# A two-part graph network on one core: transposed one-hots kept in DRAM, gathers and sums interleaved by tile, address registers loaded a group ahead

## The reference

```python
for _ in range(3):                                    # message layers, l = 0, 1, 2
    msg = silu([h[src], h[dst], edge_attr] @ W1e + b1e) @ W2e + b2e
    agg = segment_sum(msg, dst) / deg
    h = h + silu([h, agg] @ W1n + b1n) @ W2n + b2n
x = layernorm(x + h)
for W, root, b in three_relational_layers:            # l = 3, 4, 5
    seg = edge_type * n_nodes + dst
    agg = segment_sum(x[src], seg) / max(cnt, 1)
    x = x @ root + b + einsum('rni,rio->no', agg, W)  # relu after the first two
out = layernorm(x_before + x)
```

## Time and profile before

| | |
|---|---|
| median of three runs | 6398.9 us (6395.67 to 6404.14) |
| the profiled execution | 6410.94 us |
| its span in the profile | 6409.2 us |
| TensorE, VectorE busy | 5167.9 us (81%), 4519.1 us (71%) |
| ScalarE, GpSimd busy | 2721.7 us (42%), 3388.0 us (53%) |
| message layers, first gather to last sum | 765.2, 775.7 and 780.9 us |
| relational layers, likewise | 745.0, 744.5 us and a third like them |

### The profile page before, as it was taken

The page is one execution under the profiler, slowest core; times in us unless marked ns, Lnnn a source line. Parts: engine busy times, 40 slices in busy tenths (PEclk is TensorE's granted clock), DMA queues, the critical chain, the costliest instruction groups (busy, mean ns, idle before and its releaser), DMA issues.

```text
span 6409.2 us, 169000 instructions
## 1 busy us (share of the span) xinstructions
PE 5167.9 (81%) x47647; PEld 4403.8 (69%) x47651; DVE 4519.1 (71%) x10320; ACT 2721.7 (42%) x4966; POOL 3388.0 (53%) x4176
## 2 busy tenths in 40 slices
PE   3666666614888888888898888999889989899898
PEld 2444444414777767777677776888878888788887
DVE  6444444413777767767667776999969999699996
ACT  1111111124666655555555554444434444344443
POOL 1777777722555535555355553555535555355552
PEclk9999997557999999999999999999989999899997
DMA  8111111167655546555455552112211112111120
GB/s 301 29 29 29 29 29 29 29 185 208 170 168 169 170 120 169 164 165 169 121 156 168 167 168 80 57 56 57 56 34 56 57 56 57 33 57 56 56 57 26
DMA packets 376130, 639.85 MB, mean 100 GB/s; under 512 B 68352, under 2 KB 80980, under 8 KB 376075
## 3 DMA queue, kind: packets, MB, share of 16 engines
q1 hardware_dynamic: 335016, 610.44, 31.6%
q0 software_dynamic: 38400, 28.13, 2.5%
q10 hardware_dynamic: 2658, 0.51, 0.0%
HBM read 564.82 MB, written 73.22 MB: 100 GB/s over the span
## 4 chain that ended last, share of the span: by engine, by line
PE 62%; POOL 17%; issue 10%; DMA 4%; ACT 3%; another core or an unknown queue 2%; DVE 2%; POOLq 0%; SPq 0%; ACTq 0%; DVEq 0%
PE sums L870 18%; PE sums L884 15%; POOL recs L489 13%; PE gat L845 11%; PE gat L847 10%; PE gat L850 4%; POOL arena L502 3%; ACT arena L641 3%; DMA arena<-recs 2%; DMA recs<-arena 1%; PE gat L950 1%; PE gat L948 1%; PE sums L961 0%; DVE arena L1103 0%
## 5 line engine op out<-in xcount | busy, mean ns | idle before, releaser
L845 PE MATMUL gat<-table,arena 128*128 x7680 | 1918.5, 250 | 277.9 <-ACT arena L641 164.2
L502 POOL TENSOR_SCALAR arena<-iota_f,arena 128x128 f32<-128x128 f32 x1920 | 1268.5, 676 | 1315.0 <-PE sums L884 1129.1
L847 PE MATMUL gat<-table,arena 128*128 x7680 | 1924.2, 251 | 0.0
L870 PE MATMUL sums<-arena 128*128 128x192 bf16 x15360 | 1887.7, 246 | 2.0 <-DVE arena L1245 2.0
L1245 DVE TENSOR_SCALAR arena<-iota_s,meta_t 128x512 bf16<-128x512 int16 x3840 | 1531.9, 471 | 111.8 <-PE sums L870 111.8
L870 PEld LDWEIGHTS sums<-arena 128*128 128x128 bf16 x15360 | 1325.9, 98 | 2.6 <-DVE arena L1245 2.6
L641 ACT CAST arena<-gat 128x768 bf16<-128x768 f32 x960 | 767.2, 799 | 1128.1 <-PE gat L847 1128.1
L1209 DVE TENSOR_SCALAR arena<-arena,lane 128x1024 bf16<-128x1024 bf16 x1920 | 1058.1, 592 | 192.3 <-DMA arena<-rows_d 191.4
L489 POOL DMA_INDIRECT recs<-arena x800 | 950.4, 1188 | 381.0 <-issue 378.6
L884 PE MATMUL sums<-arena 128*128 128x64 f32 (+1 forms) x7680 | 959.6, 278 | 207.5 <-issue 142.2
L884 PEld LDWEIGHTS sums<-arena 128*128 128x128 f32 x7680 | 898.6, 192 | 309.7 <-issue 309.5
(11 more groups left out here) (181 smaller groups left out, 4799.9 us busy)
## 6 DMA issues: line engine op xcount, KB each, us to landing
arena<-rows_d SPq DMA_DIRECT2D x480, 512.0 KB, 4.5
arena<-recs SPq DMA_DIRECT2D x640, 272.0 KB, 2.8
arena<-rows_d SPq DMA_DIRECT2D x480, 256.0 KB, 3.3
recs<-arena SPq DMA_DIRECT2D x1, 43520.0 KB, 122.6
recs<-arena POOLq DMA_INDIRECT x800, 2.9
arena<-in_edge_attr_dram SPq DMA_DIRECT2D x100, 62.5 KB
xn<-in_x_dram SPq DMA_DIRECT2D x1, 768.0 KB
out_dram<-nodes SPq DMA_DIRECT2D x1, 768.0 KB
```

Of the source, the lines that this page charges most:

```text
L502: ins = pool.tensor_scalar(oh[u % 2][:, j, :], iota_f[:], rec_in[u][:, j, PLACE:PLACE + 1], None, ALU.is_equal)
L845: pe.matmul(at, ohT[s][:, 0, j * P:(j + 1) * P], table_flat[:, bass.ds(off[j], K3)], start=True, stop=False)
L847: ins = pe.matmul(at, ohT[s][:, 1, j * P:(j + 1) * P], table_next[:, bass.ds(off[j], K3)], start=False, stop=l >= LAYERS)
L870: ins = pe.matmul(accp[s][:, 256 * r:256 * r + K3], oh4[s][:, t, r * P:(r + 1) * P], gb[u % 4][:, t, :], start=t == 0, stop=t == GT - 1)
```

## The change

Transposed one-hots are made in layer 0 only. There SyncE stores each group's three (768 KB) to a new DRAM tensor `hots_d`, and in layers 1 to 5 it loads them instead of the rows: 768 KB per group in layers 1 and 2, 512 KB in layers 3 to 5. `ohT` has four buffers, `row_in` two. The one-hots by type and destination, `oh4`, have four buffers as well, so that `type_hots(g)` waits for the sums of `g - 4`.

TensorE runs the same `stage` in all layers: after the gathers of tile j of group g come the sums of tile j of group `g - 2`. The registers of group `g + 1` are loaded after tile 3 of group g (`load_gather`, `load_sums`), into two fixed sets. In message layers VectorE adds all three parts half by half, and the next gather waits for each half (`gat_read`) instead of for `z_ready`.

```diff
+            def store_hots(k, u):
+                sp.wait_ge(ohT_made, done(k))
+                sp.dma_start(hots_by_group[:, bass.ds(k, 1), :].rearrange("p a w -> p (a w)"),
+                             ohT[u].rearrange("p m e -> p (m e)")).then_inc(hots_stored[u], 16)
+            def load_hots(l, k, u):
+                m = 3 if l < LAYERS else 2
+                sp.wait_ge(gathered, done(2 * (l * NG + k - 4) + 1))
+                sp.dma_start(ohT[u][:, 0:m, :].rearrange("p m e -> p (m e)"),
+                             hots_by_group[:, bass.ds(k, 1), 0:m * GT * P].rearrange("p a w -> p (a w)")
+                             ).then_inc(hots_loaded[u], 16)
...
+                def load_gather(g, u, l=l):
+                    pe.load(tile_regs[u % 2], offsets[0:1, bass.ds(GT * g, GT)])
+                    if l < LAYERS:
+                        pe.load([dst_reg[u % 2]], goff[0:1, bass.ds(3 * g, 1)])
+                def load_sums(g, u, l=l):
+                    if l < LAYERS:
+                        pe.load([sum_reg[u % 2]], goff[0:1, bass.ds(3 * g + 1, 1)])
...
-                    pe.wait_ge(ohT_made, done(n))
-                    if l < LAYERS:
-                        pe.wait_ge(z_ready, done(n - 1))
...
+                    for j in range(GT):
+                        if gathers:
+                            gather_tile(g, u, j, off, dst_off)
+                        if adds:
+                            if j == 0:
+                                sums_ready(g - 2, (u + 2) % 4)
+                            sums_tile(g - 2, (u + 2) % 4, j, to)
+                        if j == 3:
+                            if gathers:
+                                load_gather(g + 1, u + 1)
+                            if not known or 1 <= g <= NG:
+                                load_sums(g - 1, u + 1)
...
-                    for k in range(1, 3):
-                        dve.wait_ge(z_step, 3 * n + 1 + k)
-                        ins = dve.tensor_tensor(z[s], z[s], parts[:, :, k * HID:(k + 1) * HID], ALU.add)
...
+                        dve.tensor_tensor(z[s][:, tiles, :], z[s][:, tiles, :], parts[:, tiles, HID:2 * HID], ALU.add
+                                          ).then_inc(z_step, 1)
+                        dve.wait_ge(z_step, 4 * n + 2 * h + 2)
+                        ins = dve.tensor_tensor(z[s][:, tiles, :], z[s][:, tiles, :], parts[:, tiles, 2 * HID:K3],
+                                                ALU.add)
+                        ins.then_inc(gat_read, 1)
...
-                    dve.wait_ge(summed, done(n - 2))
+                    dve.wait_ge(summed, done(n - 4))
```

329 lines of the change are left out of this document (172 added, 157 removed).

## The result

The changed kernel takes 6291.12 us (median of four runs, 6284.04 to 6295.09) against 6397.28 us before: a ratio of 0.9832, interval 0.9815 to 0.9849. It is faster, as forecast, but by 1.7% (106 us) and not by 314 us. The predicted time was 6085 us, and 6291 lies above the range of 5790 to 6195.

A forecast was written before the change was run, and what follows sets the result against it. VectorE was taken to bound relational layers and TensorE's sequencer, at or near its limit, message layers. Terms -306 - 32 + 18 + 6 = -314 us, from 6410.9 less 12 to the median, gave 6085 us; range 5790 to 6195.

The forecast's parts named there:

- Relational layers (-306: Layers 3 to 5: without transposed one-hots on VectorE, TensorE bounds at 4.01 us per group; -306 us over three layers.
- Layers 1 and 2 (-32: Message layers 1 and 2: sequencer still bounds, 4.65 us per group against 4.75; -16 us per layer, -32 us.
- A: The forecast: message layers unchanged or nearly so, relational layers bound by matmuls; 6085 us, 56%.
- B: Rival, message layers: register loads don't hold the sequencer, so 3.9 us per group; 5845 us, 26%.
- its sum closed on 4.67: Message group before: address instructions and register loads, with 0.82 us for the load of eight, add up to 4.67 us.
- Rival E: All layers: a register load costs by the register, eight taking 2.0 us; about 6830 us, slower, 3%.
- The prediction's sum by the 200 ns: Register loads at 200 ns per register: eight would take 1.6 us, kernel an estimated 6490 us; weighed and rejected.
- Layer 0 (+18: Layer 0: storing one-hots makes transfers the bound, 4.9 us per group; 783 us against 765, +18 us.
- part 3 of the change: Layer 0 still makes the one-hots and also stores them, 786,432 bytes per group; costed at +18 us.
- Loads of the one-hots in layers 1 and 2: Layers 1 and 2: DMA of 3.2 to 3.8 us within 4.65 per group, hidden by four buffers; cost 0.
- Rival D: Transfers bound the message layers: at 210 GB/s layer 0 +430 us, layers 1 and 2 +140; about 6640 us, 4%.
- Ends: +6: Message layers' ends: sums lag two groups, so each layer ends with one more sum alone, 2 us; +6 us in all.

## Why the prediction was right and where it was wrong

**Relational layers (-306, measured -323): right.** TensorE became the bound: busy 636.55 of 637.13 us, 3.98 us per group for 4.01, VectorE at 80%. Keeping VectorE busy brought 84 of the 108 us back; the rest of the gain is that it waits less. The load of eight was hidden at tile 3, as costed.

**Layers 1 and 2 (-32, measured -17): right on what a load does, and lucky in the sum.** That a load holds the sequencer was the open question between A and B; the records show it, and without the loads the layer takes 3.69 us per group, so it is A. But the saving was to be 0.1 us in each steady group, from 4.75 to 4.65. A steady group went from 4.74 to 4.78 us: the forecast counted the jump inside the 4.65, and with it the group is slower than before. What the layers gained lies elsewhere. Worked out from the starts of the gathers, the groups beside the regular ones cost about 10 and 14 us more in layers 1 and 2 before, where the granted clock dipped (0.98 and 0.97 of the whole window), and nothing after, at 1.00. The prediction named those dips, and did not count on their going.

The prices of the loads can be read from the records. In ns, where no stores run: 305 for one register, 546 for two, 597 for eight, 1082 for ten; and with the first word off a multiple of 16 bytes 1946 for eight and 2402 for ten. Around each load stand 0.12 us of set-up and 0.06 us after it. The table gives the groups in these terms, in us, each load counted with both (means over a layer, rounded):

| | loads | rest | group |
|---|---|---|---|
| layer 1, changed kernel | 1.74 | 3.06 | 4.80 |
| layer 1, two loads for three | 1.49 | 3.07 | 4.56 |
| layer 1, one load of ten, rows of 64 bytes | 1.28 | 3.06 | 4.34 |
| layer 1, table moved by one word | 3.10 | 3.30 | 6.40 |
| layer 2, with a store | 3.02 | 3.35 | 6.36 |
| layer 2, with a load in its place | 1.74 | 3.06 | 4.79 |
| layer 0, changed kernel | 2.39 | 3.75 | 6.14 |
| layer 0, small store | 1.74 | 3.42 | 5.16 |
| layer 0, small store and SiLU | 1.73 | 3.20 | 4.93 |
| layer 0, loads apart | 2.52 | 3.22 | 5.74 |

Where the clock stays up and nothing is stored the rest is 3.06 us whatever the loads are. The prediction's prices, which leave the set-up apart, were somewhat high: with the 0.06 us behind it a load of one is 0.36 us (it took 0.44) and the load of eight 0.66 (at most 0.82). It did not count the waits and the register arithmetic between them (0.09 to 0.22 us each in layer 1), and its sum closed on 4.67 because the 0.82 was what had been left over: a fit, and no test. Rival E's price by the register was wrong for words that lie on a multiple of 16 bytes, and its 2.0 us for eight is near what the moved table pays.

The Trainium skill (Runtime: NRT & Kernel Launch, Instruction fetch mechanics) gives about 200 ns per register for register loads out of HBM, and the Trainium skill (DMA: Bandwidth & Descriptors, Latency and other measured facts) a floor of about 600 ns for such a load. From SBUF here, one register at 0.31 us and two at 0.55 lie below that floor, so it does not hold for them. By the register, eight on a multiple of 16 bytes are far cheaper (0.60 us) and eight off it come near (1.95 us, 0.24 each). The prediction's sum by the 200 ns of the Trainium skill, 6490 us, comes to about 6460 when its own terms are added again; nothing else rests on it.

**Layer 0 (+18, measured +217): the failed step.** It is part 3 of the change. It costed the store as bytes on the DMA engines and took the largest of three limits, 4.9 us of transfers over 4.65 of sequencer. The transfers were sized right: without register loads the layer comes to 4.72 us at a DMA share of 0.96. But they were not what bound. The step took the sequencer's 4.65 us over from layers without stores, and so put what the store does to the register loads at nothing; the group took 6.14 us. The runs showed three things in its place:

- *Stores lengthen register loads.* By the means of the records the three loads take 1.87 us per group in layer 0, for 1.21 in layer 1. A store of 512 KB per group does it to layer 2 (1.21 to 2.48 us, the layer +250), a load of as many bytes does nothing, and with 1/24 of the bytes stored the load of eight is back at 0.60 us and layer 0 takes 157 us less. Layer 0 without register loads loses 227 us though all is stored. Whether the store's reading of SBUF or its writing to DRAM does it was not tried.
- *The clock.* The long idle stretch, over 2 us where layer 1 has 0.9, is followed by tiles at the lower level. TensorE is busy 111 us longer than with small stores; busy time isn't lost time, and loads placed apart gave 64 us back at a clock of 0.95. This part depends on the first.
- *ScalarE's table loads*, 2.57 us in every fourth group, were hidden behind VectorE and stand in the sums' chain now that the sums come two groups after the gathers. They cost 36 us where the stores are small and about 15 us in the changed kernel. The prediction did not look at ScalarE's chain in layer 0. The Trainium skill (ScalarE activation tables: per-element evaluation and per-set limits, Table sets in the compiler and the runtime) says that the back end places table loads block by block. The runs fit that: the loop of layer 0 repeats both of its loads in each turn (80 in all, and none in the loops of layers 1 and 2), and one SiLU ahead of it took them out.

By the table, the 1.34 us between a group of layer 1 and one of layer 0 are 0.65 in the loads and 0.69 in the rest. Of the rest, 0.36 is there with small stores too, 0.22 of it the table loads; 0.33 comes with the full stores, at the lower clock. Of the 60 us that remain of the 217 when little is stored (825 for 765), 36 are the tables; the other 21 to 24 stay open.

**Loads of the one-hots in layers 1 and 2: hidden, right.** They land in 4.2 us, and even at a share of 0.92 layer 2 kept its time. Rival D was wrong in its mechanism, transfers as the bound, but its sign, stores that cost more than their bytes, was what happened, in layer 0 alone. **Ends: +6** is inside the layers' times and was not seen apart.

The signs named beforehand worked: "if the share is well below that and the group is at 4.65, the term of +18 is wrong" is half of what the window of layer 0 shows; the share is 0.79, and the group is at 6.14 instead of 4.65.

## What to carry to other kernels

Where a sequencer is the bound, look for its register loads in the trace by their source line: the page counts no time for them, but their records have lengths. Begin the words of each on a multiple of 16 bytes, since that mattered most here, then make the loads fewer, then place them apart, so that they don't leave the engine idle for 2 to 3 us at once. When a forecast compares a group before and after, let both count the same things (here the jump), and look afterwards at a steady group as well as at the layer. When a change moves work from one engine to another, follow the chain of each engine through the layer anew: what was hidden behind a slow one (here table loads) may stand in the way afterwards. A limit read in one stage holds in another only if what runs beside it is the same; a stage that gets a new store deserves a range that says so.

## What was not expected of the hardware

- A load of eight registers from SBUF on TensorE's sequencer takes 0.60 us when its first word lies on a multiple of 16 bytes from the start of the table, and 1.95 when it lies 4 bytes further. Rows of 48 bytes are as good as rows of 64 (1.08 us for ten registers in both), rows of 44 are not (2.40 in three groups of four). An estimate from the six medians above, which it gives within 0.02 us: 0.30 us for the first register or for each four that start on such a multiple, and 0.235 for every other one. Why this is so was not tried.
- Stores of 512 to 768 KB per group lengthen these loads, up to 2.6 us for one, at a DMA share of 0.8; a load of 512 KB at 0.92 does not.
- TensorE, idle for 0.9 us in each 4.65, kept a granted clock of 1.00; idle for about 2 to 3 us in every second group, it was granted 0.84 to 0.85 on average.
